# Spreading the FP4 quantizer over two engines step by step, and grouping the layer-norm apply of an MLP, in an eight-core transformer kernel

## The chip, the cores and the metric

The kernel runs on the 8 cores of one Trainium2 chip. Each core handles one of the 8 batch elements on its own, with no exchange between cores. The metric is the device time in microseconds (us) of the slowest core. Engines: PE (TensorE), DVE (VectorE), ACT (ScalarE), POOL (GpSimd), SP (SyncE, which here only issues transfers).

## What is computed

Two transformer layers on x of 2048 x 1024 per core. Layer 0 adds to x a differential attention and a gated FFN whose three products take FP4-quantized operands. Layer 1 adds a linear attention and a two-deep local-attention FFN block with an MLP. The parts that matter here are the quantizer, which runs on blocks of 16 values, and the layer norm ahead of each MLP:

```python
def fp4_quant_dequant(x):
    xb = x.reshape(shape[:-1] + (shape[-1] // 16, 16))
    scale = max(max(abs(xb)) / 6.0, 1e-12)          # one per block of 16
    idx = searchsorted(_MID, abs(xb / scale))       # grid 0 .5 1 1.5 2 3 4 6
    return (_GRID[idx] * sign(xb) * scale).reshape(shape)
# layer 0 FFN: everything that enters a product is quantized
gate = fp4(x) @ fp4(w_gate).T;  y = fp4(x) @ fp4(w_up).T
out  = fp4(silu(gate) * y) @ fp4(w_down).T
# layer 1, before each of the two MLPs (h is the token-shifted x)
h = (h - mu) / sqrt(var + 1e-5) * lg + lb
```

## The kernel before

The program is written by hand with counting semaphores. `Sem.inc` adds one when an instruction completes, `Sem.wait` makes an engine's queue wait until the count is reached, and `drain()` holds an engine's queue until its earlier instructions are done. The stages follow each other with barriers between them; within a stage most steps wait for the step before.

`emit_quant(k, S, Q)` (L266 to L320) quantizes one tile S of 128 x W into Q. It keeps three wide buffers, `qA`, `qB`, `qC` (each 128 x 2816 f32, used as f32 or as bf16 halves), and three short ones, `qbm`, `qib6`, `qbm12`, with one entry for each block of 16. In order: L275 DVE maximum of each block; L277 a floor on it; L279 reciprocal; L280 the block's scale (times 1/6); L282 the reciprocal times 6; L285 A = S times that; L287 B = A clamped to +-2; L288 C = A clamped to +-4; L291 POOL C + A; L293 A = 0.5 C + B; L296 z, rounded by adding and subtracting a large constant, in bf16; L301, L302, L303 three simple functions of z (m1, c6, z2); L305 m1 limited; L307 s1 = m1 + c6; L310 psi = z2 - s1; L317 POOL Q = psi times the block's scale. So two of the instructions are POOL's and sixteen are DVE's, with a DVE drain between dependent ones.

It is called 164 times:

- 16 times with W = 1024 in the loop over x tiles in `emit_l0`, then 16 PE transposes of the tile with its bf16 copy (`emit_transposes`, L330 PE, L332 DVE copy), then the next tile;
- 44 times with W = 1024 and 8 times with W = 2816 in `emit_l0_wquant` (weights). Each turn loads a row block (SP, L878), quantizes it, transposes it and stores it (L891); the next load waits for the stores' data to be ready and for DVE and POOL, and goes into the same buffer `WLD`;
- 80 times with W = 512 and 16 times with W = 256 in `emit_l0_ffn`. For each column chunk `oc` and row tile `j4` 16 matmuls (8 of L930, 8 of L933) are followed by a silu (ACT, L937), a product (DVE, L939), the quantizer into `HQB`, and 4 or 2 transposes. The next 16 matmuls wait for all of it.

Together that is 129,024 columns (60 x 1024 + 80 x 512 + 16 x 256 + 8 x 2816).

In `emit_l1f_mlp` (run for l = 0 and 1) the layer norm is applied for each half `hf` and each 512 columns `tc`: three short matmuls (L1687 to L1691) spread the mean and the scale of each token over the partitions in PSUM; then for each of 8 feature tiles `ft` DVE multiplies into a temporary T1 (L1696), DVE adds (L1699), and ACT applies gain and bias into `XHh` (L1702). DVE waits for ACT before the next `ft`, since T1 is one buffer. PE and POOL stand at a later barrier or wait.

Of the kernel before, what the change touches and what calls it, by code (L numbers as in the profile page):

```python
# [127 lines left out]
def full_barrier(k, engines="tvsg", dma=True):  # L128
    s = k.s_x
    if "t" in engines:  # L130
        s.inc(k.te.drain())
    if "v" in engines:
        s.inc(k.ve.drain())
    if "s" in engines:
        s.inc(k.se.drain())
    if "g" in engines:
        s.inc(k.ge.drain())
    for e in (k.te, k.ve, k.se, k.ge, k.sy):
        e.wait_ge(s.h, s.n)
        if dma and engines == "tvsg":  # L140
            for sem in (k.s_ld, k.s_la, k.s_lb, k.s_lg, k.s_lh, k.s_lc, k.s_st, k.s_dmp):
                sem.wait(e)
# [122 lines left out]

def emit_quant(k, S, Q, ge_q=True):  # L266
    v, g = k.ve, k.ge
    k.s_g.wait(v)
    W = S.shape[-1]
    nb = W // 16  # L270
    A, B, C = k.qA, k.qB, k.qC
    Ab, Bb, Cb = k.qAb, k.qBb, k.qCb
    bm, ib6, bm12 = k.qbm, k.qib6, k.qbm12
    S3 = S.rearrange("p (a b) -> p a b", b=16)
    v.tensor_reduce(bm[:, 0:nb], S3, axis=AX.X, op=ALU.max, apply_absolute_value=True)  # L275
    v.drain()
    v.tensor_scalar(bm[:, 0:nb], bm[:, 0:nb], 6e-12, None, op0=ALU.max)  # L277
    v.drain()
    v.reciprocal(ib6[:, 0:nb], bm[:, 0:nb])  # L279
    v.tensor_scalar(bm12[:, 0:nb], bm[:, 0:nb], k.rc6[:, 0:1], None, op0=ALU.mult)  # L280
    v.drain()
    v.tensor_scalar(ib6[:, 0:nb], ib6[:, 0:nb], 6.0, None, op0=ALU.mult)  # L282
    v.drain()
    ib6b = ib6[:, 0:nb].unsqueeze(2).broadcast_to((128, nb, 16))
    v.tensor_tensor(A[:, 0:W].rearrange("p (a b) -> p a b", b=16), S3, ib6b, op=ALU.mult)  # L285
    v.drain()
    v.tensor_scalar(B[:, 0:W], A[:, 0:W], -2.0, 2.0, op0=ALU.max, op1=ALU.min)  # L287
    v.tensor_scalar(C[:, 0:W], A[:, 0:W], -4.0, 4.0, op0=ALU.max, op1=ALU.min)  # L288
    k.s_v.inc(v.drain())  # L289
    k.s_v.wait(g)  # L290
    k.s_g.inc(g.tensor_tensor(C[:, 0:W], C[:, 0:W], A[:, 0:W], op=ALU.add))  # L291
    k.s_g.wait(v)
    v.scalar_tensor_tensor(A[:, 0:W], C[:, 0:W], 0.5, B[:, 0:W], op0=ALU.mult, op1=ALU.add)  # L293
    v.drain()
    z = Bb[:, 0:W]
    v.tensor_scalar(z, A[:, 0:W], k.mcol[:, 0:1], k.mcol[:, 0:1],  # L296
                    op0=ALU.add, op1=ALU.subtract)
    v.drain()
    m1, c6 = Cb[:, 0:W], Ab[:, 0:W]
    z2, s1 = Ab[:, W:2 * W], Cb[:, W:2 * W]  # L300
    v.tensor_scalar(m1, z, 0.5, -2.0, op0=ALU.mult, op1=ALU.max)  # L301
    v.tensor_scalar(c6, z, -6.0, 6.0, op0=ALU.max, op1=ALU.min)  # L302
    v.tensor_scalar(z2, z, 2.0, None, op0=ALU.mult)  # L303
    v.drain()
    v.tensor_scalar(m1, m1, 2.0, None, op0=ALU.min)  # L305
# [9 lines left out]
    if ge_q:
        k.s_v.wait(g)
        k.s_g.inc(g.tensor_tensor(Q3, psi3, bm12b, op=ALU.mult))  # L317
    else:
        v.tensor_tensor(Q3, psi3, bm12b, op=ALU.mult)
        k.s_v.inc(v.drain())  # L320


def emit_transposes(k, pairs, identity):
# [57 lines left out]
def emit_l0(k, h, out_h):  # L381
# [23 lines left out]
    for j in range(NT):  # L405
# [14 lines left out]
        k.s_v.wait(se)  # L420
        k.s_s.inc(se.activation(XB, XNT, AF.Copy, bias=0.0))
        emit_quant(k, XNT, XQT)
        if DEV_STAGE == "xq":
            k.s_g.wait(ge)
# [441 lines left out]
def emit_l0_wquant(k, h, WLD, WQB, STG):  # L866
    te, ve, se, ge, sy = k.te, k.ve, k.se, k.ge, k.sy
    specs = [(h["wg0"], h["wqgT_s"], 22, 1024),
             (h["wu0"], h["wquT_s"], 22, 1024),
             (h["wd0"], h["wdqT_s"], 8, 2816)]  # L870
    for src, dst, nrt, W in specs:
        srcr = src.rearrange("(r p) w -> p r w", p=128)
        dstr = dst.rearrange("(bb p) o -> p bb o", p=128)
        nb = W // 128
        for r in range(nrt):
            k.s_v.wait(sy)
            k.s_g.wait(sy)
# [236 lines left out]
def emit_l1_ffn(k, h, out_h, XINT):  # L1114
# [439 lines left out]
def emit_l1f_mlp(k, h, out_h, XINT, l, LNGC, LNBC, B1AC, B1GC, st4):  # L1554
    te, ve, se, ge, sy = k.te, k.ve, k.se, k.ge, k.sy
# [98 lines left out]
    w1src = h["w1"][l].rearrange("(a p) o -> p a o", p=128)  # L1654
    GH = k.qCb[:, 4096:4608]
    AT = k.qCb[:, 4608:5120]
    T1 = k.qCb[:, 5120:5632]

    for hf in range(2):
        ar.mark()  # L1660
        XHh = ar.bf(8, 1024)
        ar.mark()
        XFMh = ar.bf(8, 1032)
# [19 lines left out]
        for tc in range(2):  # L1683
            gcol = 1024 * hf + 512 * tc
            te.wait_ge(k.s_v.h, k.s_v.n)
            te.wait_ge(k.s_s.h, k.s_s.n)
            k.s_mm.inc(te.matmul(k.psB[:, 2, :], k.ones1b[0:1, 0:128],  # L1687
                                 IVB[0:1, gcol:gcol + 512], start=True, stop=True))
            te.matmul(k.psB[:, 3, :], k.ones1b[0:1, 0:128],
                      CHB[0:1, gcol:gcol + 512], start=True, stop=False)  # L1690
            k.s_mm.inc(te.matmul(k.psB[:, 3, :], k.ones1b[0:1, 0:128],  # L1691
                                 CLB[0:1, gcol:gcol + 512], start=False, stop=True))
            k.s_mm.wait(ve)
            for ft in range(8):
                soff = 1 if ft < 4 else 0
                ve.tensor_tensor(T1, XFMh[:, ft, soff + 512 * tc: soff + 512 * tc + 512],  # L1696
                                 k.psB[:, 2, :], op=ALU.mult)
                ve.drain()
                ve.tensor_tensor(T1, T1, k.psB[:, 3, :], op=ALU.add)  # L1699
                k.s_v.inc(ve.drain())  # L1700
                k.s_v.wait(se)
                k.s_s.inc(se.activation(XHh[:, ft, 512 * tc:512 * tc + 512], T1, AF.Identity,  # L1702
                                        scale=LNGC[:, ft:ft + 1], bias=LNBC[:, ft:ft + 1]))
                k.s_s.wait(ve)
        full_barrier(k, "tvs")
        ar.release()
        AHq = ar.bf(22, 512)
# [2 lines left out]
        for qt in range(2):  # L1710
# [3 lines left out]
            for hc in range(22):  # L1714
                ocw = 128 if hc < 21 else 42
                b = hc % 2
# [8 lines left out]
                for ag in range(2):  # L1725
                    for ic in range(8):
# [8 lines left out]
                              bias=B1GC[0:ocw, hc:hc + 1])  # L1735
                se.activation(AT[0:ocw, :], k.psA[0:ocw, 0, :], AF.Identity,
                              bias=B1AC[0:ocw, hc:hc + 1])
# [3 lines left out]
                                           op=ALU.mult))  # L1741
# [132 lines left out]
```

## Time and profile before

| | us |
|---|---|
| median of the runs shown (12597.27 to 12635.81) | 12616.54 |
| time of the profiled execution | 12579.73 |
| span of the profiled execution, slowest core | 12577.8 |
| busy: PE / DVE / ACT / POOL | 4373.9 / 3686.7 / 1556.9 / 1112.6 |

The eight cores span 12539.7 to 12577.8 us. No engine is busy for more than 35% of the span. The page has the busy time of each engine, the span in 40 slices, the transfer queues, the chain of work that ended last, and the costliest groups of instructions; the trace behind it can be asked for single stretches, lines and shapes.

### The profile page before, as it was taken

What the parts mean: (1) busy time and instruction counts of PE and PEld (TensorE: products, weight loads), DVE (VectorE), ACT (ScalarE), POOL (GpSimd) and SP (SyncE); (2) the same over time, 40 slices, a digit from 0 to 9 for tenths busy, and PEclk for the clock granted to TensorE, in tenths of its full rate; (3) what the DMA queues carried; (4) which work ended last, traced back from release to release, by engine and by line L of the source; (5) the groups of instructions that cost most, each with busy time, mean ns of one, the idle gap of its engine ahead of it and who ended that gap; (6) DMA issues with size and microseconds to landing.
All of it is one profiled execution on the core that took longest, in us unless ns stands there. A gap on an engine that the chain in (4) does not pass through costs nothing.

```text
span 12577.8 us, 70640 instructions; the slowest of 8 cores (12539.7 to 12577.8 us)
## 1 busy us (share of the span) xinstructions
PE 4373.9 (35%) x17918; PEld 1725.2 (14%) x18113; DVE 3686.7 (29%) x9617; ACT 1556.9 (12%) x2754; POOL 1112.6 (9%) x925
## 2 busy tenths in 40 slices
PE   1000033443444423333243333244446233244443
PEld 0000011111111111111121111111112011111111
DVE  6544533111111232332323544400100644400100
ACT  1000012333333100000011111100001111100100
POOL 1111210000000010110100000011111000011110
PEclk9999995555555666666666555577677555676676
DMA  1111110000000201011031000133233000233233
GB/s 52 30 36 35 43 33 1 0 0 0 0 0 0 65 20 44 29 35 37 27 87 58 6 0 1 27 32 34 23 31 28 2 1 0 31 30 32 27 29 69
DMA packets 563397, 326.69 MB, mean 26 GB/s; under 512 B 467046, under 2 KB 519398, under 8 KB 561980
## 3 DMA queue, kind: packets, MB, share of 16 engines
q0 software_dynamic: 406448, 125.85, 9.7%
q1 hardware_dynamic: 156564, 196.32, 4.8%
q8 instruction: 167, 2.74, 0.1%
q14 instruction: 218, 1.79, 0.0%
HBM read 388.63 MB, written 50.92 MB: 35 GB/s over the span
## 4 chain that ended last, share of the span: by engine, by line
PE 31%; DVE 22%; DMA 15%; issue 7%; POOL 7%; ACT 6%; ACTq 5%; DVEq 5%; SPq 0%; POOLq 0%; PEldq 0%
PE psA L1727 8%; DMA ARENA<-w 7%; PE psB L726 4%; ACTq L712 3%; PE psB L1755 3%; PE psA L930 2%; POOL qC L291 2%; DVE qB L1388 2%; PE psA L933 2%; DMA ARENA<-wquT_s 2%; DMA ARENA<-x_s 2%; POOL ARENA L1740 2%; DVE ARENA L1481 1%; ACT ARENA L711 1%; PE psB L1479 1%
## 5 line engine op out<-in xcount | busy, mean ns | idle before, releaser
L1727 PE MATMUL psA<-ARENA 128*128 128x512 bf16 (+1 forms) x2760 | 963.5, 522 | 1647.1 <-DMA ARENA<-w 1639.8
L330 PE MATMUL psA<-c_idb,ARENA 128*128 128x128 bf16 x1424 | 244.3, 264 | 1948.5 <-POOL ARENA L317 1605.0
L1761 DVE TENSOR_TENSOR ARENA<-ARENA,psB 128x512 bf16<-128x512 bf16 x64 | 41.1, 684 | 2891.3 <-PE psB L1755 2891.3
L726 PE MATMUL psB<-ARENA 128*65 128x512 bf16 (+3 forms) x1280 | 522.2, 562 | 825.3 <-ACTq L712 509.2
L711 ACT ACTIVATE ARENA<-psA 128x512 bf16<-128x512 f32 (+3 forms) x1280 | 578.9, 539 | 920.5 <-PE psA L703 920.2
L1727 PEld LDWEIGHTS psA<-ARENA 128*128 128x128 bf16 (+1 forms) x2816 | 343.7, 127 | 2267.5 <-issue 2170.8
L291 POOL TENSOR_TENSOR qC<-qC,qA 128x512 f32<-128x512 f32 (+3 forms) x164 | 301.4, 1838 | 2409.4 <-DVEq L289 2409.4
L717 DVE TENSOR_TENSOR ARENA<-ARENA,c_m 128x512 bf16<-128x512 bf16 x128 | 54.5, 426 | 1553.8 <-ACTq L712 1553.8
L1479 PE MATMUL psB<-c_idb,ARENA 128*128 128x128 bf16 x1120 | 226.1, 270 | 654.8 <-DVEq L1469 504.0
L330 PE MATMUL psA<-c_idb,qC 128*128 128x128 bf16 x352 | 60.2, 265 | 1066.0 <-POOL qC L317 1065.8
L330 PEld LDWEIGHTS psA<-c_idb,ARENA 128*128 128x128 bf16 x1424 | 148.5, 104 | 2045.4 <-issue 2009.7
L1734 ACT ACTIVATE qC<-psA,B1GC 128x512 bf16<-128x512 f32 (+1 forms) x176 | 120.9, 687 | 2481.1 <-PE psA L1727 2481.1
L332 DVE COPY ARENA<-psA 128x128 bf16<-128x128 bf16 x1776 | 288.3, 221 | 444.0 <-PE psA L330 415.9
L930 PE MATMUL psA<-ARENA 128*128 128x512 bf16 (+1 forms) x752 | 303.1, 576 | 301.8 <-DMA ARENA<-wquT_s 262.3
L1740 POOL TENSOR_TENSOR ARENA<-qC 128x512 bf16<-128x512 bf16 (+1 forms) x176 | 201.2, 1143 | 2224.2 <-ACTq L1738 2224.2
L1755 PE MATMUL psB<-ARENA 128*128 128x512 bf16 (+1 forms) x1376 | 332.6, 391 | 3.0 <-issue 1.6
L726 PEld LDWEIGHTS psB<-ARENA 128*65 128x65 bf16 x1280 | 170.6, 162 | 1186.4 <-issue 1175.3
L1460 ACT ACTIVATE ARENA<-psA,stats 128x640 bf16<-128x640 f32 (+4 forms) x256 | 172.1, 723 | 1136.2 <-DVEq L1456 1136.2
L939 DVE TENSOR_TENSOR qA<-qA,psA 128x512 f32<-128x512 f32 (+1 forms) x96 | 61.7, 643 | 833.0 <-ACT qA L937 833.0
L937 ACT ACTIVATE qA<-psA 128x512 f32<-128x512 f32 (+1 forms) x96 | 53.9, 561 | 1987.8 <-PE psA L933 1987.8
L1481 DVE COPY ARENA<-psB 128x128 bf16<-128x128 bf16 x1120 | 206.7, 221 | 236.1 <-PE psB L1479 232.3
L293 DVE SCALAR_TENSOR_TENSOR qA<-qC,qB 128x512 f32<-128x512 f32 (+3 forms) x164 | 160.5, 978 | 349.0 <-POOL qC L291 349.0
(345 smaller groups left out, 7236.7 us busy)
## 6 DMA issues: line engine op xcount, KB each, us to landing
ARENA<-w POOLq DMA_DIRECT2D x336, 256.0 KB, 4.7
ARENA<-x_s SPq DMA_DIRECT2D x80, 512.0 KB, 3.6
x_s<-ARENA SPq DMA_DIRECT2D x48, 512.0 KB
ARENA<-wqgT_s SPq DMA_DIRECT2D x20, 1024.0 KB, 5.5
ARENA<-wquT_s SPq DMA_DIRECT2D x20, 1024.0 KB, 8.0
ARENA<-x_in SPq DMA_DIRECT2D x32, 512.0 KB, 3.9
ARENA<-wg SPq DMA_DIRECT2D x22, 512.0 KB, 4.0
ARENA<-wu SPq DMA_DIRECT2D x22, 512.0 KB, 4.0
```

Source lines behind the costliest of these rows:

```text
L291: k.s_g.inc(g.tensor_tensor(C[:, 0:W], C[:, 0:W], A[:, 0:W], op=ALU.add))
L330: k.s_mm.inc(k.te.transpose(pv, src, identity))
L332: k.s_v.inc(ve.tensor_copy(dst, pv))
L711: se.activation(UT[:, jj, off:512], k.psA[:, jj, off:512], AF.Exp)
L712: k.s_s.inc(se.drain())
L726: k.s_mm.inc(te.matmul(k.psB[0:65, jj, off:512], VT[:, kt, kvv, 0:65], UT[:, jj, off:512], start=(kt == 0), stop=(kt == nkt - 1)))
L930: te.matmul(k.psA[:, 0, 0:ocw], XQF[:, ic, 128 * j:128 * j + 128], WGS[:, ic, 0:ocw], start=(ic == 0), stop=(ic == 7))
L1479: k.s_mm.inc(te.transpose(pvb, UT[:, jj, 128 * b:128 * b + 128], k.idb[:]))
L1481: k.s_v.inc(ve.tensor_copy(UTT[:, jj, ktr, 128 * lq:128 * lq + 128], pvb))
L1727: mm = te.matmul(k.psA[0:ocw, ag, :], W1S[:, ag, b, ic, 0:ocw], XHh[:, ic, toff:toff + 512], start=(ic == 0), stop=(ic == 7))
L1740: k.s_g.inc(ge.tensor_tensor(AHq[0:ocw, hc, :], AT[0:ocw, :], GH[0:ocw, :], op=ALU.mult))
L1755: mm = te.matmul(pb, AHq[0:kcw, hc, 128 * tch:128 * tch + 128], W2R[0:kcw, hc, 512 * dc:512 * dc + 512], start=False, stop=(hc == 21))
```

## The change

In `emit_quant` the steps go to DVE and POOL in turn. Each step waits for the other engine's last one and signals its own completion directly; the DVE drains inside are gone. The floor, the block scale, B, m1, z2 and s1 move from DVE to POOL; the multiplication of the reciprocal by 6 is folded into the instruction that makes A; and a POOL memset of one column is put in to keep the turns. s1 moves from `qC`'s second half to `qB`'s. In the MLP's layer norm the eight `ft` are handled in three passes (8 multiplies, 8 adds, 8 ACT instructions) through `XHh` in place of T1.

```diff
-    v.tensor_reduce(bm[:, 0:nb], S3, ...)
-    v.drain()
-    v.tensor_scalar(bm[:, 0:nb], bm[:, 0:nb], 6e-12, None, op0=ALU.max)
...
+    def vstep(fn):
+        v.wait_ge(k.s_g.h, k.s_g.n)
+        k.s_v.inc(fn())
+    def gstep(fn):
+        g.wait_ge(k.s_v.h, k.s_v.n)
+        k.s_g.inc(fn())
+    vstep(lambda: v.tensor_reduce(bm[:, 0:nb], S3, axis=AX.X, op=ALU.max,
+                                  apply_absolute_value=True))
+    gstep(lambda: g.tensor_scalar(bm[:, 0:nb], bm[:, 0:nb], 6e-12, None, op0=ALU.max))
+    vstep(lambda: v.reciprocal(ib6[:, 0:nb], bm[:, 0:nb]))
+    gstep(lambda: g.tensor_scalar(bm12[:, 0:nb], bm[:, 0:nb], 1.0 / 6.0, None, op0=ALU.mult))
+    vstep(lambda: v.scalar_tensor_tensor(A, S3, 6.0, ib6b, op0=ALU.mult, op1=ALU.mult))
+    gstep(lambda: g.tensor_scalar(B[:, 0:W], A[:, 0:W], -2.0, 2.0, op0=ALU.max, op1=ALU.min))
+    vstep(lambda: v.tensor_scalar(C[:, 0:W], A[:, 0:W], -4.0, 4.0, op0=ALU.max, op1=ALU.min))
+    gstep(lambda: g.tensor_tensor(C[:, 0:W], C[:, 0:W], A[:, 0:W], op=ALU.add))
+    vstep(lambda: v.scalar_tensor_tensor(A[:, 0:W], C[:, 0:W], 0.5, B[:, 0:W], ...))
+    gstep(lambda: g.memset(k.smallc[:, 14:15], 0.0))
+    vstep(lambda: v.tensor_scalar(z, A[:, 0:W], k.mcol[:, 0:1], k.mcol[:, 0:1], ...))
+    gstep(lambda: g.tensor_scalar(m1, z, 0.5, -2.0, op0=ALU.mult, op1=ALU.max))
+    vstep(lambda: v.tensor_scalar(c6, z, -6.0, 6.0, op0=ALU.max, op1=ALU.min))
+    gstep(lambda: g.tensor_scalar(z2, z, 2.0, None, op0=ALU.mult))
+    vstep(lambda: v.tensor_scalar(m1, m1, 2.0, None, op0=ALU.min))
+    gstep(lambda: g.tensor_tensor(s1, m1, c6, op=ALU.add))
+    vstep(lambda: v.tensor_tensor(psi, z2, s1, op=ALU.subtract))
+    gstep(lambda: g.tensor_tensor(Q3, psi3, bm12b, op=ALU.mult))
...
             for ft in range(8):
-                ve.tensor_tensor(T1, XFMh[...], k.psB[:, 2, :], op=ALU.mult)
-                ve.drain()
-                ve.tensor_tensor(T1, T1, k.psB[:, 3, :], op=ALU.add)
-                k.s_v.inc(ve.drain())
-                k.s_v.wait(se)
-                k.s_s.inc(se.activation(XHh[...], T1, AF.Identity, scale=..., bias=...))
-                k.s_s.wait(ve)
+                ve.tensor_tensor(XHh[...], XFMh[...], k.psB[:, 2, :], op=ALU.mult)
+            ve.drain()
+            for ft in range(8):
+                ve.tensor_tensor(XHh[...], XHh[...], k.psB[:, 3, :], op=ALU.add)
+            k.s_v.inc(ve.drain())
+            k.s_v.wait(se)
+            for ft in range(8):
+                se.activation(XHh[...], XHh[...], AF.Identity, scale=..., bias=...)
+            k.s_s.inc(se.drain())
+            k.s_s.wait(ve)
+            k.s_s.wait(te)
```

## Rows read from the trace of the kernel before

**Rows 1.** Busy time by stage (windows): weight quantizing, then one FFN group of four tiles.

```profile
core 6: us, PE busy (x) PEld busy (x) DVE busy (x) ACT busy (x) POOL busy (x), PEclk, DMA share, GB/s
385.00:1357.00 972.00, 59.28 (x352) 36.64 (x352) 483.33 (x1056) 0.00 (x0) 186.84 (x88) 1.00 0.12 35
4300.00:4840.00 540.00, 185.00 (x636) 75.48 (x648) 171.70 (x504) 14.76 (x25) 54.99 (x52) 0.63 0.13 36
```

**Rows 2.** Timeline of one W = 1024 quantizing: start us, us, engine, line.

```profile
519.56 1.22 DVE L275 TENSOR_REDUCE qbm<-ARENA 128x64 f32<-128x1024 f32 x1 [5.08 <-DMA ARENA<-wg]
...
521.12 0.55 DVE L279 RECIPROCAL qib<-qbm 128x64 f32<-128x64 f32 x1
...
522.10 1.23 DVE L285 TENSOR_TENSOR qA<-ARENA,qib 128x1024 f32<-128x1024 f32 x1
523.40 0.69 DVE L287 TENSOR_SCALAR qB<-qA 128x1024 f32<-128x1024 f32 x1
524.01 0.69 DVE L288 TENSOR_SCALAR qC<-qA 128x1024 f32<-128x1024 f32 x1
524.87 2.34 POOL L291 TENSOR_TENSOR qC<-qC,qA 128x1024 f32<-128x1024 f32 x1 [12.63 <-DVEq L289]
527.31 1.23 DVE L293 SCALAR_TENSOR_TENSOR qA<-qC,qB 128x1024 f32<-128x1024 f32 x1 [2.62 <-POOL qC L291]
...
529.50 0.43 DVE L301 TENSOR_SCALAR qC<-qB 128x1024 bf16<-128x1024 bf16 x1
...
530.68 0.43 DVE L305 TENSOR_SCALAR qC<-qC 128x1024 bf16<-128x1024 bf16 x1
531.18 0.69 DVE L307 TENSOR_TENSOR qC<-qC,qA 128x1024 bf16<-128x1024 bf16 x1
531.95 0.69 DVE L310 TENSOR_TENSOR qC<-qA,qC 128x1024 bf16<-128x1024 bf16 x1
532.81 1.91 POOL L317 TENSOR_TENSOR ARENA<-qC,qbm 128x1024 bf16<-128x1024 bf16 x1 [5.61 <-DVEq L311]
```

**Rows 3.** Groups by shape, POOL's two lines: xcount, busy us, mean ns, idle before.

```profile
L317 POOL TENSOR_TENSOR ARENA<-qC,qbm 128x1024 bf16<-128x1024 bf16 x60 | 114.6, 1909 | 337.3 <-DVEq L311 337.3
L317 POOL TENSOR_TENSOR qC<-qC,qbm 128x512 bf16<-128x512 bf16 x80 | 83.7, 1046 | 300.6 <-DVEq L311 300.6
L291 POOL TENSOR_TENSOR qC<-qC,qA 128x2816 f32<-128x2816 f32 x8 | 48.9, 6108 | 205.8 <-DVEq L289 205.8
L317 POOL TENSOR_TENSOR ARENA<-qC,qbm 128x2816 bf16<-128x2816 bf16 x8 | 39.5, 4932 | 97.5 <-DVEq L311 97.5
```

**Rows 4.** Groups by shape, two of DVE's clamping lines at W = 2816.

```profile
L287 DVE TENSOR_SCALAR qB<-qA 128x2816 f32<-128x2816 f32 x8 | 13.0, 1627 | 0.6
L301 DVE TENSOR_SCALAR qC<-qB 128x2816 bf16<-128x2816 bf16 x8 | 7.2, 894 | 0.6
```

**Rows 5.** Timeline: a DVE copy that releases POOL directly, and POOL's one-output iota.

```profile
6773.21 0.21 DVE L1195 COPY E2B<-psA 2x128 bf16<-2x128 bf16 x1 [0.55 <-PE psA L1193]
6773.56 1.84 POOL L1201 IOTA qA<- 128x2048 f32 x1 [3.46 <-DVE E2B L1195]
```

**Rows 6.** Timeline of the first layer-norm apply (512 columns, eight feature tiles).

```profile
8091.06 0.69 DVE L1696 TENSOR_TENSOR qC<-ARENA,psB 128x512 bf16<-128x512 bf16 x1 [1.79 <-PE psB L1691]
...
8093.56 0.69 DVE L1696 TENSOR_TENSOR qC<-ARENA,psB 128x512 bf16<-128x512 bf16 x1 [1.04 <-ACT ARENA L1702]
...
8110.08 0.81 ACT L1702 ACTIVATE ARENA<-qC,LNBC,LNGC 128x512 bf16<-128x512 bf16 x1 [1.68 <-DVEq L1700]
```

**Rows 7.** Timeline: four DVE products in a row, and four ACT instructions in a row.

```profile
7032.63 2.48 DVE L1398 TENSOR_TENSOR ARENA<-ARENA,psA 128x512 bf16<-128x512 bf16 x4 [2.14 <-PE psA L1394]
```

```profile
2339.00 2.06 ACT L711 ACTIVATE ARENA<-psA 128x512 bf16<-128x512 f32 x4 [3.29 <-PE psA L703]
```

**Rows 8.** Timeline of PE in one FFN burst of 16 matmuls.

```profile
4516.47 3.57 PE L930 MATMUL psA<-ARENA 128*128 128x512 bf16 x8 [0.48 <-DVE ARENA L332]
4519.84 2.05 PE L933 MATMUL psA<-ARENA 128*128 128x512 bf16 x8
```

**Rows 9.** PE in two stretches of that burst: busy us (xcount), granted clock, DMA.

```profile
4516.50:4519.50 3.00, 3.00 (x8) 0.50 0.00 0
4520.00:4522.00 2.00, 1.89 (x9) 0.96 0.00 0
```

More of the change, by code:

```diff
@@ L267, in emit_quant @@
     v, g = k.ve, k.ge
-    k.s_g.wait(v)
     W = S.shape[-1]
@@ L274, in emit_quant @@
     S3 = S.rearrange("p (a b) -> p a b", b=16)
-    v.tensor_reduce(bm[:, 0:nb], S3, axis=AX.X, op=ALU.max, apply_absolute_value=True)
-    v.drain()
-    v.tensor_scalar(bm[:, 0:nb], bm[:, 0:nb], 6e-12, None, op0=ALU.max)
[L278 to L283, printed above, removed]
-    ib6b = ib6[:, 0:nb].unsqueeze(2).broadcast_to((128, nb, 16))
@@ L285, in emit_quant @@
[L285 to L293, printed above, removed]
@@ L294, in emit_quant @@
-    v.drain()
-    z = Bb[:, 0:W]
[L296 to L305, printed above, removed]
@@ L306, in emit_quant @@
-    v.drain()
-    v.tensor_tensor(s1, m1, c6, op=ALU.add)
-    v.drain()
+    def vstep(fn):
[8 more added lines that the diff above has]
+    vstep(lambda: v.reciprocal(ib6[:, 0:nb], bm[:, 0:nb]))
@@ new lines, in emit_quant @@
+    gstep(lambda: g.tensor_scalar(bm12[:, 0:nb], bm[:, 0:nb], 1.0 / 6.0, None, op0=ALU.mult))
+    ib6b = ib6[:, 0:nb].unsqueeze(2).broadcast_to((128, nb, 16))
+    vstep(lambda: v.scalar_tensor_tensor(A[:, 0:W].rearrange("p (a b) -> p a b", b=16),
+                                         S3, 6.0, ib6b, op0=ALU.mult, op1=ALU.mult))
+    gstep(lambda: g.tensor_scalar(B[:, 0:W], A[:, 0:W], -2.0, 2.0, op0=ALU.max, op1=ALU.min))
+    vstep(lambda: v.tensor_scalar(C[:, 0:W], A[:, 0:W], -4.0, 4.0, op0=ALU.max, op1=ALU.min))
@@ new lines, in emit_quant @@
+    gstep(lambda: g.tensor_tensor(C[:, 0:W], C[:, 0:W], A[:, 0:W], op=ALU.add))
+    vstep(lambda: v.scalar_tensor_tensor(A[:, 0:W], C[:, 0:W], 0.5, B[:, 0:W],
+                                         op0=ALU.mult, op1=ALU.add))
+    gstep(lambda: g.memset(k.smallc[:, 14:15], 0.0))
+    z = Bb[:, 0:W]
+    vstep(lambda: v.tensor_scalar(z, A[:, 0:W], k.mcol[:, 0:1], k.mcol[:, 0:1],
+                                  op0=ALU.add, op1=ALU.subtract))
+    m1 = Cb[:, 0:W]
+    c6 = Ab[:, 0:W]
+    z2 = Ab[:, W:2 * W]
@@ L309, in emit_quant @@
+    s1 = Bb[:, W:2 * W]
+    gstep(lambda: g.tensor_scalar(m1, z, 0.5, -2.0, op0=ALU.mult, op1=ALU.max))
[3 more added lines that the diff above has]
+    gstep(lambda: g.tensor_tensor(s1, m1, c6, op=ALU.add))
     psi = Cb[:, 0:W]
-    v.tensor_tensor(psi, z2, s1, op=ALU.subtract)
-    k.s_v.inc(v.drain())
+    vstep(lambda: v.tensor_tensor(psi, z2, s1, op=ALU.subtract))
@@ L314, in emit_quant @@
     psi3 = psi.rearrange("p (a b) -> p a b", b=16)
[L315 to L320, printed above, removed]
+    gstep(lambda: g.tensor_tensor(Q3, psi3, bm12b, op=ALU.mult))
 def emit_transposes(k, pairs, identity):
@@ L1656, in emit_l1f_mlp @@
     AT = k.qCb[:, 4608:5120]
-    T1 = k.qCb[:, 5120:5632]
     for hf in range(2):
@@ L1695, in emit_l1f_mlp @@
                 soff = 1 if ft < 4 else 0
-                ve.tensor_tensor(T1, XFMh[:, ft, soff + 512 * tc: soff + 512 * tc + 512],
+                ve.tensor_tensor(XHh[:, ft, 512 * tc:512 * tc + 512],
+                                 XFMh[:, ft, soff + 512 * tc: soff + 512 * tc + 512],
                                  k.psB[:, 2, :], op=ALU.mult)
-                ve.drain()
-                ve.tensor_tensor(T1, T1, k.psB[:, 3, :], op=ALU.add)
-                k.s_v.inc(ve.drain())
-                k.s_v.wait(se)
-                k.s_s.inc(se.activation(XHh[:, ft, 512 * tc:512 * tc + 512], T1, AF.Identity,
-                                        scale=LNGC[:, ft:ft + 1], bias=LNBC[:, ft:ft + 1]))
-                k.s_s.wait(ve)
+            ve.drain()
+            for ft in range(8):
+                ve.tensor_tensor(XHh[:, ft, 512 * tc:512 * tc + 512],
+                                 XHh[:, ft, 512 * tc:512 * tc + 512],
+                                 k.psB[:, 3, :], op=ALU.add)
+            k.s_v.inc(ve.drain())
+            k.s_v.wait(se)
+            for ft in range(8):
+                se.activation(XHh[:, ft, 512 * tc:512 * tc + 512],
+                              XHh[:, ft, 512 * tc:512 * tc + 512], AF.Identity,
+                              scale=LNGC[:, ft:ft + 1], bias=LNBC[:, ft:ft + 1])
+            k.s_s.inc(se.drain())
+            k.s_s.wait(ve)
+            k.s_s.wait(te)
         full_barrier(k, "tvs")
```

## Prediction

> **What bounds the kernel now.** I read first the page's busy shares and its 40 slices, to see whether an engine is full. None is. Then the windows by stage: while the weights are quantized DVE is busy for 483 of 972 us and POOL for 187; in an FFN group PE has 185 of 540 us, DVE 172, POOL 55 [rows 1]. The stages are chains in which one engine works at a time. Then the timeline of one quantizing, which the reader should follow row by row: DVE works from 519.56 to 524.70, POOL to 527.21, DVE to 532.64, POOL to 534.72, and no two rows overlap by more than the tail of a DVE instruction [rows 2]. This piece is 15.16 us long. The code says what stands around it: the transposes wait for Q, the next load into the one buffer WLD or the next 16 matmuls wait for the transposes. Nothing is prepared meanwhile, so whatever a quantizing gains or loses goes 164 times straight into the end.
>
> **Boundaries.** From one DVE instruction over a drain to the next takes 0.07 us (L305 ends at 531.11, L307 starts at 531.18). DVE through a drain to POOL takes 0.17 (L288 ends 524.70, L291 starts 524.87), POOL to DVE 0.10 (527.21 to 527.31) [rows 2]. A DVE instruction that releases POOL by itself, as the new code has it, is shown once: 0.14 (6773.42 to 6773.56) [rows 5].
>
> **The quantizer, W = 1024.** I count what leaves, what comes, and the boundaries.
>
> Leaving DVE: the floor L277, 521.12 - 519.56 - 1.22 - 0.07 = 0.27. L280 and L282, 522.10 - 521.12 - 0.55 - 0.07 = 0.36. B (L287), 524.01 - 523.40 = 0.61. m1 and z2: from L301 to L305 is 1.18, of which c6 with a boundary keeps 0.49, so 0.69. s1 (L307), 531.95 - 531.18 = 0.77 [rows 2]. Together 2.70.
>
> Coming to POOL: s1 has L317's shape and types, 1.91 [rows 2]. The other five have no row: nowhere does POOL run an operation with one input and a constant. What is known of POOL is two-input work: 4932 ns at 2816 columns and 1909 at 1024, so 1.69 ns a column and 0.18 us fixed in bf16; 6108 and 2340 in f32, so 2.10 ns a column and the same 0.18 [rows 2, 3]; and work with no input, iota, (1.84 - 0.18) / 2048 = 0.81 ns a column [rows 5]. These are the bounds of a one-input operation. I take half the two-input rate, 1.05 ns in f32 and 0.84 in bf16: it reads half as much, and the result lies next to iota, which shows that POOL's writing and looping can go at that pace. Then B costs 0.18 + 1.08 = 1.26, m1 and z2 1.04 each, the two on 64 columns 0.25 each, the memset the fixed 0.18. With s1: 1.26 + 2.08 + 0.50 + 0.18 + 1.91 = 5.93.
>
> The Trainium skill (GPSIMD Engine Reference, section 3.1) gives a port-bound POOL loop of up to two operations 1.03 cycles an element, and a tight loop otherwise 1.8; at the 1.2 GHz it states these are 0.86 and 1.5 ns. By the first the term below for all calls would be some 25 us smaller, by the second some 230 us larger (estimates from that page). No row here shows either.
>
> Boundaries: before, between the instructions that stay, seven of 0.07, two of 0.17, one of 0.10, 0.93 in all. After, 18 instructions in strict turns have 17: nine DVE to POOL at 0.14 and eight back at 0.10, 2.06. That is 1.13 more. Dropping drains thus gains nothing; a turn costs more than a drain.
>
> The balance is 5.93 - 2.70 + 1.13 = +4.36 us a quantizing. No cover exists for it: each POOL step is waited for by the next DVE step, even where the data don't ask for it (B and C could run side by side, and so could m1, c6 and z2), and behind DVE's waits stand the transposes' copies.
>
> **Other widths.** Per column come 1.05 + 0.84 + 0.84 + 1.69, and 2 x 1.05 / 16 for the short ones: 4.55 ns. Per column leave (1627 - 694) / 1792 = 0.52 for B and the same for s1, (894 - 427) / 1792 = 0.26 each for m1 and z2 [rows 2, 4], and 3 x 0.52 / 16 = 0.10: 1.66 ns. The net is 2.89 ns a column, and per call 4.36 - 1024 x 0.00289 = 1.40 us. Over 164 calls and 129,024 columns: 230 + 373 = +603 us.
>
> **The layer norm.** Eight feature tiles take 8110.89 - 8091.06 = 19.83 us, 2.50 each [rows 6]. After, a pass of 8 DVE instructions goes at (2.48 - 0.69) / 3 = 0.60 from start to start [rows 7]: 7 x 0.60 + 0.69 = 4.89, twice, with a drain 9.85, then 0.17 to ACT. ACT's steps lie between 0.51 (2.06 / 4) [rows 7] and the 0.81 of a lone one [rows 6]; with 0.70, 0.81 + 7 x 0.70 = 5.7. That is 15.7, or -4.1 us, and there are 8 such pieces (2 layers, 2 halves, 2 chunks): -33 us (-43 to -27). PE waits for this stretch before and after, so the gain counts in full; the added wait on PE is for work that it needed anyway. What follows is the barrier and the first weight load, which start that much sooner.
>
> **Sum.** +603 - 33 = +570 us. The profiled execution took 12579.7, so it would take 13150; the median of the runs shown is 37 us above it, so I say 12616.5 + 570, rounded to 13185.
>
> **Rivals.**
>
> 1. POOL's one-input operations go no faster than its two-input ones, because the pace is set by its loop and not by what it reads. Then B costs 1.05 ns a column more, m1 and z2 0.85 each, the short ones 0.13: 2.88 x 129,024 = +371, in all +941, 13560 us. For it speaks that the f32 and bf16 rates differ by less than the bytes do (2.10 against 1.69) [rows 2, 3]; against it that iota shows a pace of 0.81. The skill's 1.8 cycles would lie between this and my value. 24%.
>
> 2. The clock. An FFN burst starts at a granted clock of 0.50 (the 1.2 GHz level) and reaches 0.96 (2.4 GHz nearly throughout) in its second half [rows 9]. If the longer pause of PE kept the low level through the burst, its 16 matmuls would take 16 x 3.37 / 8 = 6.7 us in place of 5.42 [rows 8], 1.3 x 80 = +105 us, 13290. Against it: the clock is already at the low level when the burst starts, so 2.7 us more of pause have nothing to take away. 8%.
>
> 3. The other side, not slower: POOL does what it is given at DVE's price, s1 included. Then 0.69 + 0.43 + 0.42 + 0.69 + 0.36 for the short ones + 0.18 come, 2.77, and the balance is 2.77 - 2.70 + 1.13 = 1.20 us a call with hardly a part per column: 197 - 33 = +164, 12780 us, within 2%. It would need the total below +252 (2%). With only B, m1 and z2 at DVE's rates the total is still 570 - (0.53 + 0.58 + 0.58) x 129,024 / 1000 = +352, so the decision lies with s1, and POOL's 1.91 for that shape is a row [rows 3]. 4%.
>
> That the quantizer is not on the path, so that only the -33 remains, is excluded by rows 2: DVE's next row waits for each POOL row.
>
> **How the numbers follow.** 62% for my case, with a spread of its own: low end, all at iota's pace (-39), every boundary 0.10 (-59), memset free (-30), layer norm -43: 13050; high end, pieces of rival 1. 24, 8 and 4% for the rivals, 2% for something unseen. The range is 13040 to 13560, from just below my low end up to rival 1 (with boundaries of 0.17 that one would reach 13610). It leaves out rival 3 and the far edge of rival 1. 2% is about what a measurement of this kernel can tell from no change. Slower by over 2%: 0.94, within 2%: 0.05, faster: 0.01.
>
> **What would show it.** After: six POOL lines more, each in a gap of DVE's; the time from block maximum to Q at W = 1024 about 19.5 us; POOL clamp of 1024 f32 columns 1.26 us (2.34 by rival 1, 0.69 by rival 3); bursts in the FFN that still end at the high clock; layer-norm pieces of 15.7 us. POOL's busy time should rise by some 800 us and DVE's fall by some 400. I am wrong if the clamp's price is far from 1.26, or if a turn costs much else than 0.10 to 0.14.

## The result and the profile after

The changed kernel takes 14077.29 us in the median (14036.59 to 14144.68) against 12605.12 for the kernel before: a ratio of 1.1164, 95% interval 1.1131 to 1.1196. That is +1472 us, where +570 was forecast, and outside the range. The direction and the place were right, the size was not.

First the stretches, which answer to [rows 1]. The same core, 6, in both kernels: weight quantizing from its first quantizer to the first projection matmul, the FFN, and everything from the first layer-norm piece to the end. Columns are the stretch, its length, busy us (and count) of PE, PE's weight loads, DVE, ACT, POOL, then the granted clock and the transfers.

Kernel before:

```profile
65.00:1786.00 1721.00, 132.96 (x784) 81.59 (x784) 921.39 (x1904) 23.49 (x21) 346.90 (x139) 1.00 0.13 37
4311.00:6494.00 2183.00, 734.52 (x2544) 301.65 (x2592) 706.35 (x2038) 75.07 (x131) 222.40 (x211) 0.64 0.13 38
8091.00:12578.00 4487.00, 1810.43 (x6532) 706.59 (x6633) 792.68 (x2075) 450.19 (x702) 524.20 (x545) 0.67 0.25 26
```

Kernel after:

```profile
62.00:2711.00 2649.00, 132.80 (x784) 81.72 (x784) 733.09 (x1428) 23.49 (x21) 1395.62 (x615) 1.00 0.08 24
5211.00:7959.00 2748.00, 711.47 (x2544) 296.88 (x2592) 559.66 (x1366) 75.09 (x131) 865.56 (x883) 0.63 0.11 30
9557.00:13998.00 4441.00, 1799.14 (x6532) 705.21 (x6633) 781.19 (x2075) 444.63 (x702) 524.73 (x545) 0.67 0.25 26
```

The two stretches with the quantizer grew by 928 and 565 us, 1493 together; on the other seven cores, cut at the same instructions, by 1496 to 1529. In the first, POOL's busy time rose by 1049 us and DVE's fell by only 188. That makes 861, and the hand-overs add some 77 (68 calls of 1.13 us each, an estimate by the prediction's count): the stretch grew by 928, since nobody works beside POOL.

The last stretch shrank by 46 on this core, but it can't be read as the layer norm's gain. On cores 4 to 7 it shrank by 43 to 50 us, at a granted clock of 0.67 (0.66 to 0.67 before); on cores 0 to 3 it grew by 10 to 32, at 0.65 (0.66 to 0.67 before). What the layer norm gives is shown by its pieces below and by e1_ln_alone.

Then one W = 1024 quantizing of the kernel after, which answers to [rows 2] (start us, us, engine, line; in brackets the idle time before it and who ended it):

```profile
571.75 1.22 DVE L283 TENSOR_REDUCE qbm<-ARENA 128x64 f32<-128x1024 f32 x1 [4.03 <-DMA ARENA<-wg]
573.13 0.37 POOL L285 TENSOR_SCALAR qbm<-qbm 128x64 f32<-128x64 f32 x1 [8.90 <-DVE qbm L283]
...
576.17 3.63 POOL L291 TENSOR_SCALAR qB<-qA 128x1024 f32<-128x1024 f32 x1 [1.48 <-DVE qA L289]
579.91 0.69 DVE L292 TENSOR_SCALAR qC<-qA 128x1024 f32<-128x1024 f32 x1 [3.89 <-POOL qB L291]
580.75 2.34 POOL L293 TENSOR_TENSOR qC<-qC,qA 128x1024 f32<-128x1024 f32 x1 [0.95 <-DVE qC L292]
583.19 1.23 DVE L294 SCALAR_TENSOR_TENSOR qA<-qC,qB 128x1024 f32<-128x1024 f32 x1 [2.59 <-POOL qC L293]
584.54 0.10 POOL L296 MEMSET smallc<- 128x1 f32 x1 [1.45 <-DVE qA L294]
584.75 0.81 DVE L298 TENSOR_SCALAR qB<-qA,c_mcol 128x1024 bf16<-128x1024 f32 x1 [0.33 <-POOL smallc L296]
585.72 3.63 POOL L304 TENSOR_SCALAR qC<-qB 128x1024 bf16<-128x1024 bf16 x1 [1.08 <-DVE qB L298]
589.46 0.43 DVE L305 TENSOR_SCALAR qA<-qB 128x1024 bf16<-128x1024 bf16 x1 [3.90 <-POOL qC L304]
590.04 2.77 POOL L306 TENSOR_SCALAR qA<-qB 128x1024 bf16<-128x1024 bf16 x1 [0.69 <-DVE qA L305]
...
593.50 2.11 POOL L308 TENSOR_TENSOR qB<-qC,qA 128x1024 bf16<-128x1024 bf16 x1 [0.68 <-DVE qC L307]
595.72 0.69 DVE L310 TENSOR_TENSOR qC<-qA,qB 128x1024 bf16<-128x1024 bf16 x1 [2.37 <-POOL qB L308]
596.55 1.91 POOL L314 TENSOR_TENSOR ARENA<-qC,qbm 128x1024 bf16<-128x1024 bf16 x1 [0.94 <-DVE qC L310]
```

From 571.75 to 598.46 it is 26.71 us, against 15.16. The reader should look at three durations, 3.63, 3.63 and 2.77 us for B, m1 and z2, and then at the bracket of the DVE row behind each (3.89, 3.90 and 3.03): DVE stands for that time and the two hand-overs. The turns are as expected: 0.15 us from DVE to POOL (580.60 to 580.75), 0.10 back (583.09 to 583.19).

The groups by shape give POOL's price at W = 2816 (count, busy us, mean ns, idle before):

```profile
L291 POOL TENSOR_SCALAR qB<-qA 128x2816 f32<-128x2816 f32 x8 | 77.4, 9675 | 26.8 <-DVE qA L289 26.8
L306 POOL TENSOR_SCALAR qA<-qB 128x2816 bf16<-128x2816 bf16 x8 | 58.5, 7310 | 9.5 <-DVE qA L305 9.5
L308 POOL TENSOR_TENSOR qB<-qC,qA 128x2816 bf16<-128x2816 bf16 x8 | 43.9, 5492 | 9.2 <-DVE qC L307 9.2
```

With the 1024 rows: (9675 - 3630) / 1792 = 3.37 ns a column for two operations, (7310 - 2770) / 1792 = 2.53 for one, both above the 2.10 of two-input f32 work [rows 2, 3].

Last the first layer-norm piece, which answers to [rows 6]:

```profile
9611.74 4.87 DVE L1689 TENSOR_TENSOR ARENA<-ARENA,psB 128x512 bf16<-128x512 bf16 x8 [1.79 <-PE psB L1684]
9616.69 4.87 DVE L1694 TENSOR_TENSOR ARENA<-ARENA,psB 128x512 bf16<-128x512 bf16 x8
9621.69 5.74 ACT L1700 ACTIVATE ARENA<-ARENA,LNBC,LNGC 128x512 bf16<-128x512 bf16 x8 [50.46 <-DVEq L1697]
```

It ends at 9627.43, 15.69 us after its start, as forecast (15.7), with each of its three terms in place.

### The profile page after: what moved, and what is told of

Read it like the earlier page. It is cut to its first block, busy times and chain, and to the rows that moved or that the text cites. A ratio compares the mean times of both kernels' runs of the same rounds, so it can differ in the third digit from the quotient of the medians.

```text
span 14143.1 us, 70955 instructions; the slowest of 8 cores (13997.7 to 14143.1 us)
## 1 busy us (share of the span) xinstructions
PE 4485.3 (32%) x18113; PEld 1742.9 (12%) x18113; DVE 3339.6 (24%) x8469; ACT 1551.9 (11%) x2754; POOL 2802.2 (20%) x2073
## 4 chain that ended last, share of the span: by engine, by line
PE 29%; POOL 18%; DVE 18%; DMA 13%; issue 7%; ACTq 5%; ACT 5%; DVEq 4%; POOLq 0%; SPq 0%; PEldq 0%
PE psA L1728 7%; DMA ARENA<-w 6%; PE psB L720 4%; POOL qC L304 3%; POOL qB L291 3%; ACTq L706 3%; PE psB L1756 3%; POOL qA L306 3%; POOL qC L293 2%; PE psA L924 2%; POOL qB L308 2%; DVE qB L1382 1%; POOL ARENA L1741 1%; DMA ARENA<-wquT_s 1%; DMA ARENA<-x_s 1%
## 5 line engine op out<-in xcount | busy, mean ns | idle before, releaser
L1728 PE MATMUL psA<-ARENA 128*128 128x512 bf16 (+1 forms) x2816 | 1001.4, 534 | 1618.0 <-DMA ARENA<-w 1618.0
L291 POOL TENSOR_SCALAR qB<-qA 128x512 f32<-128x512 f32 (+3 forms) x164 | 466.2, 2843 | 204.0 <-DVE qA L289 204.0
L304 POOL TENSOR_SCALAR qC<-qB 128x512 bf16<-128x512 bf16 (+3 forms) x164 | 466.8, 2846 | 158.4 <-DVE qB L298 158.4
L285 POOL TENSOR_SCALAR qbm<-qbm 128x32 f32<-128x32 f32 (+3 forms) x164 | 54.4, 331 | 1842.7 <-DVE qbm L283 1842.7
L924 PE MATMUL psA<-ARENA 128*128 128x512 bf16 (+1 forms) x768 | 298.8, 566 | 297.1 <-DMA ARENA<-wquT_s 260.6
L306 POOL TENSOR_SCALAR qA<-qB 128x512 bf16<-128x512 bf16 (+3 forms) x164 | 357.7, 2181 | 104.0 <-DVE qA L305 104.0
L1756 PE MATMUL psB<-ARENA 128*128 128x512 bf16 (+1 forms) x1408 | 372.6, 423 | 0.0
```

The lines of the kernel that those rows point to most:

```text
L291: gstep(lambda: g.tensor_scalar(B[:, 0:W], A[:, 0:W], -2.0, 2.0, op0=ALU.max, op1=ALU.min))
L304: gstep(lambda: g.tensor_scalar(m1, z, 0.5, -2.0, op0=ALU.mult, op1=ALU.max))
L306: gstep(lambda: g.tensor_scalar(z2, z, 2.0, None, op0=ALU.mult))
L924: te.matmul(k.psA[:, 0, 0:ocw], XQF[:, ic, 128 * j:128 * j + 128], WGS[:, ic, 0:ocw], start=(ic == 0), stop=(ic == 7))
L1728: mm = te.matmul(k.psA[0:ocw, ag, :], W1S[:, ag, b, ic, 0:ocw], XHh[:, ic, toff:toff + 512], start=(ic == 0), stop=(ic == 7))
L1756: mm = te.matmul(pb, AHq[0:kcw, hc, 128 * tch:128 * tch + 128], W2R[0:kcw, hc, 512 * dc:512 * dc + 512], start=False, stop=(hc == 21))
```

## The experiments

Theory P: the excess is what POOL asks for one-input operations. Theory T: it is the price of handing every step over. All ratios are to the kernel before, timed on the same chip as the experiment.

### The layer norm alone (e1_ln_alone)

```diff
 # emit_quant as before; only the layer norm is the changed kernel's
```

> The quantizer of before with the grouped layer norm of after. The changed kernel's trace has one layer-norm piece at 15.69 us against 19.83 before. If nothing takes that back, eight pieces give -33 us: about 12572 against a before of 12605, ratio 0.997. Rival: the gain is lost in the weight loads and the barrier behind it, ratio 1.000.

Measured: 12544.71 against 12575.67 us, ratio 0.997 (0.9954 to 0.9986). The gain is real: the interval is 18 to 58 us, and the 33 read from the timeline lie in it. So what stands behind the layer norm did not take all of it back.

### Turns without moving any work (e2_turns)

The edit, shortened:

```diff
-    v.drain()                       # ten times in emit_quant
+    k.s_v.inc(last)                 # last: the DVE instruction before
+    g.wait_ge(k.s_v.h, k.s_v.n)
+    k.s_g.inc(g.memset(k.smallc[:, 14:15], 0.0))
+    v.wait_ge(k.s_g.h, k.s_g.n)
```

> The kernel before, except that each of the 10 DVE drains inside the quantizer is replaced by a turn over POOL (DVE releases POOL, POOL sets one column to zero, DVE waits for it). Every computing instruction stays on its engine. Theory P (the loss of the change is what POOL asks for one-input operations): a turn costs 0.14 + 0.10 + 0.10 us in place of 0.07, so 10 x 0.27 x 164 = +440 us, ratio about 1.035. Theory T (the loss of about 1500 us is the price of the turns, 17 a call, so 0.54 us each): 10 x 0.54 x 164 = +885 us, ratio about 1.07.

Measured: 12989.11 us, ratio 1.0335 (1.0313 to 1.0357). Its timeline around A (L291 there) and B (L293):

```profile
551.58 1.23 DVE L291 TENSOR_TENSOR qA<-ARENA,qib 128x1024 f32<-128x1024 f32 x1 [0.32 <-POOL smallc L277]
552.93 0.10 POOL L277 MEMSET smallc<- 128x1 f32 x1 [1.45 <-DVE qA L291]
553.13 0.69 DVE L293 TENSOR_SCALAR qB<-qA 128x1024 f32<-128x1024 f32 x1 [0.32 <-POOL smallc L277]
```

From the end of A (552.81) to B is 0.32 us where a drain took 0.07. Ten times 164 times 0.25 is 410 us, and 0.0335 x 12576 is 421. A turn has the price that the rows of before gave it (0.14 + 0.10 for the hand-overs). Theory T, which needed 1.07, is out.

### One-input work back on DVE, turns kept (e3_one_input_on_dve)

The edit, shortened:

```diff
-    gstep(lambda: g.tensor_scalar(B[:, 0:W], ...))
+    gstep(lambda: g.memset(k.smallc[:, 14:15], 0.0))
+    v.wait_ge(k.s_g.h, k.s_g.n)
+    v.tensor_scalar(B[:, 0:W], ...)      # m1 and z2 likewise, ahead of c6
```

> The changed kernel with B, m1 and z2 back on DVE; where they stood POOL sets one column to zero, so the number of turns is the same. Theory P: at W = 1024 POOL's 3.63 + 3.63 + 2.77 us give way to 0.61 + 0.34 + 0.34 on DVE and three times 0.10, -8.4 us; over all widths about -1070 us, to 13010, ratio 1.032 to before. Theory T: the turns are all still there, so it stays within some 300 us of the changed kernel, ratio 1.09 or more.

Measured: 12979.82 us, ratio 1.0319 (1.0302 to 1.0337), the figure of theory P. Three of POOL's instructions, taken away with all the turns left standing, return 1.1164 - 1.0319 = 0.0845 of the time of before, some 1065 of the 1472 us. This one and e2_turns settle where the time went.

### What POOL charges (e4_prices, e8_prices2)

In both, lone POOL operations, nearly all on 128 x 1024, are put ahead of the changed kernel; nothing reads their results. Six of e4_prices' fifteen, with the lines they have in the profile:

```diff
+    gs(lambda: g.tensor_scalar(c, a, -2.0, 2.0, op0=ALU.max, op1=ALU.min))   # L1832
+    gs(lambda: g.tensor_scalar(c, a, -2.0, None, op0=ALU.max))               # L1833
+    gs(lambda: g.tensor_scalar(c, a, 2.0, None, op0=ALU.mult))               # L1834
+    gs(lambda: g.tensor_scalar(c, a, 2.0, 1.0, op0=ALU.mult, op1=ALU.add))   # L1835
+    gs(lambda: g.tensor_copy(c, a))                                          # L1836
...
+    gs(lambda: g.tensor_tensor(c, a, a, op=ALU.add))                         # L1839
...
```

> The changed kernel with a list of lone POOL operations on 128 x 1024 ahead of it (three times each, some 110 us longer for it). From 3.37 ns a column with two operations and 2.53 with one: if each arithmetic operation costs 0.84 ns on top of a base, a plain copy costs 0.18 + 1.7 = 1.9 us, a lone max and a lone multiply both 2.77, and f32 and bf16 the same. Rival: what is paid for is the way of the instruction (a constant operand), then a copy goes at iota's 0.8 ns a column, 1.0 us, and only instructions with constants are slow. z + z as a two-input sum: about 2.1 us in bf16 against 2.77 for z times 2.

Groups by shape of e4_prices:

```profile
L1832 POOL TENSOR_SCALAR qC<-qA 128x1024 f32<-128x1024 f32 x3 | 10.9, 3623 | 22.7 <-DVEq L133 22.4 <-POOL qC L1832 0.3
L1834 POOL TENSOR_SCALAR qC<-qA 128x1024 f32<-128x1024 f32 x3 | 8.3, 2769 | 0.5 <-POOL qC L1834 0.3 <-POOL qC L1833 0.2
L1833 POOL TENSOR_SCALAR qC<-qA 128x1024 f32<-128x1024 f32 x3 | 8.3, 2764 | 0.5 <-POOL qC L1833 0.3 <-POOL qC L1832 0.2
...
L1839 POOL TENSOR_TENSOR qC<-qA 128x1024 f32<-128x1024 f32 x3 | 5.7, 1891 | 0.4
...
L1835 POOL TENSOR_SCALAR qC<-qA 128x1024 f32<-128x1024 f32 x3 | 3.1, 1045 | 0.5 <-POOL qC L1835 0.3 <-POOL qC L1834 0.2
L1836 POOL COPY qC<-qA 128x1024 f32<-128x1024 f32 x3 | 3.1, 1039 | 0.4
```

A lone max and a lone multiply cost the same 2.77 us; max and min together 3.62. But multiply and add together cost 1.04, less than the multiply alone, and as much as a copy. So neither the expectation (a base and 0.84 ns for each operation, a copy of 1.9 us) nor its rival (every instruction with a constant is slow) held. The second list, given here in words, looks for the bounds of the quick case:

```text
op0, op1 on f32 unless said:  L1831 mult, mult    L1832 add, mult
L1833 add, add    L1834 mult, subtract    L1835 mult, max
L1836 add    L1837 min    L1838 mult, add in bf16    L1839 the same, f32 to bf16
L1840 mult, add on 2816 columns    L1841 mult by a constant held in memory
```

> The changed kernel with a second list of lone POOL operations ahead of it. If only multiply then add is quick, the pairs mult-mult, add-mult, add-add, mult-subtract take 3.6 us and lone add and min 2.77; if all pairs without max or min are quick, they take 1.04. Multiply and add in bf16, f32 to bf16, and on 2816 f32 columns: 1.04, 1.04 and 2.6 us (0.84 ns a column) if the quick way does not depend on type. A constant taken from memory in place of the instruction: 2.77, as the lone multiply.

```profile
L1834 POOL TENSOR_SCALAR qC<-qA 128x1024 f32<-128x1024 f32 x3 | 10.9, 3634 | 0.5 <-POOL qC L1834 0.3 <-POOL qC L1833 0.2
L1833 POOL TENSOR_SCALAR qC<-qA 128x1024 f32<-128x1024 f32 x3 | 10.9, 3632 | 0.5 <-POOL qC L1833 0.3 <-POOL qC L1832 0.2
...
L1840 POOL TENSOR_SCALAR qC<-qA 128x2816 f32<-128x2816 f32 x3 | 7.6, 2538 | 0.5 <-POOL qC L1840 0.3 <-POOL qC L1839 0.2
...
L1838 POOL TENSOR_SCALAR qC<-qA 128x1024 bf16<-128x1024 bf16 x3 | 3.1, 1045 | 0.5 <-POOL qC L1838 0.3 <-POOL qC L1837 0.2
...
L1832 POOL TENSOR_SCALAR qC<-qA 128x1024 f32<-128x1024 f32 x3 | 3.1, 1043 | 0.5 <-POOL qC L1832 0.3 <-POOL qC L1831 0.2
L1831 POOL TENSOR_SCALAR qC<-qA 128x1024 f32<-128x1024 f32 x3 | 3.1, 1040 | 19.7 <-DVEq L133 19.4 <-POOL qC L1831 0.3
```

Quick are multiply-add, multiply-multiply and add-multiply in f32, and multiply-add in bf16 too (the other two were not tried in it); from the two widths of multiply-add, (2538 - 1045) / 1792 = 0.83 ns a column. Slow at 3.6 us are add-add and multiply-subtract, and multiply-max, which is m1's pair (3626 ns here). Lone add and min cost 2.77, a lone multiply by a constant from memory 2.84. Both parts of the expectation missed: it is not the pair multiply then add alone, and it is not all pairs without max or min. Why it is these three pairs is left open.

### The quick pair in the kernel (e7_z2_mult_add)

```diff
-    gstep(lambda: g.tensor_scalar(z2, z, 2.0, None, op0=ALU.mult))
+    gstep(lambda: g.tensor_scalar(z2, z, 2.0, 0.0, op0=ALU.mult, op1=ALU.add))
```

> The changed kernel with one edit: POOL makes z2 as z times 2 plus 0 (two operations) where it made z times 2 (one). If POOL's lone multiply and add pair is quick in bf16 as it was in f32 (1.04 us at 1024 columns, against 2.77 for the lone multiply), -1.73 us at W = 1024 and about -220 us in all, ratio 1.099. If the price goes by the number of operations, it becomes 3.63 us and the kernel 110 us longer, ratio 1.125.

Measured: 13859.13 us, ratio 1.1026 (1.0992 to 1.106). z2 at W = 1024:

```profile
L306 POOL TENSOR_SCALAR qA<-qB 128x1024 bf16<-128x1024 bf16 x60 | 62.8, 1047 | 41.6 <-DVE qA L305 41.6
```

An addition of zero takes z2 from 2771 to 1047 ns, and over all widths POOL's time for z2 from 357.7 to 139.2 us. The difference of the ratios, 0.0138, is 174 us with about 60 either way; the 220 expected is within that.

### Waits only where data ask (e5_data_waits)

The edit in words:

```diff
-    vstep / gstep in strict turns
+    each instruction on the engine it has in the changed kernel, but
+    B (POOL) beside C (DVE), bm12 beside the reciprocal, m1 beside c6,
+    z2 beside the limit on m1; no memset
```

> The changed kernel with every instruction on the engine that the change gave it, but with waits only where data ask for them, so that B runs beside C, the block scale beside the reciprocal, m1 beside c6, z2 beside the limit on m1; the memset is gone. From the rows of the changed kernel that hides at W = 1024 some 0.95 + 0.58 + 0.69 + 0.69 us and saves 0.28, -3.2 us; over all widths about -480 us, so 13600, ratio 1.08. Rival: a DVE instruction and a POOL instruction do not run side by side (the later one stands until the first is done), then only the turns are saved, about -150 us, ratio 1.105. In the trace: whether C (0.69 us alone) ends long before B or with it.

Measured: 13703.05 us, ratio 1.0889 (1.0858 to 1.092): 0.0275, or 347 us, come back, not 480. The engines do run side by side, but not freely:

```profile
598.11 0.69 DVE L296 TENSOR_SCALAR qC<-qA 128x1024 f32<-128x1024 f32 x1
598.16 4.13 POOL L294 TENSOR_SCALAR qB<-qA 128x1024 f32<-128x1024 f32 x1 [1.58 <-DVE qA L291]
...
610.81 2.77 POOL L312 TENSOR_SCALAR qA<-qB 128x1024 bf16<-128x1024 bf16 x1
610.95 1.18 DVE L316 TENSOR_SCALAR qC<-qC 128x1024 bf16<-128x1024 bf16 x1 [3.60 <-POOL qC L310]
```

B, started 0.05 us behind C, takes 4.13 us and not 3.63. The limit on m1, started behind z2, takes 1.18 and not 0.43. The one that starts second pays. How much it pays depends on the width. At W = 2816 the same pair of z2 and the limit on m1 reads:

```profile
2492.95 7.30 POOL L312 TENSOR_SCALAR qA<-qB 128x2816 bf16<-128x2816 bf16 x1
2493.08 7.92 DVE L316 TENSOR_SCALAR qC<-qC 128x2816 bf16<-128x2816 bf16 x1 [9.64 <-POOL qC L310]
```

By the Trainium skill (SBUF — State Buffer, section "Who interferes with whom") the ports that POOL shares with a DVE instruction in a 2-port mode go to whoever issues first, and the second "fully blocks" for the whole instruction. At W = 2816 this agrees: DVE's instruction (0.89 us alone) takes 7.92 and ends 0.75 us behind POOL's. POOL behind DVE agrees too: B grows by 0.49 us behind a C of 0.69 and by 1.44 behind one of 1.63, each time some 0.15 us less than the rest of DVE's instruction. But at W = 1024 DVE's ended 1.45 us ahead of POOL's, so there it did not wait for the whole of it. Why the narrower tile gets through is left open.

POOL's B and m1 are longer by 60 and 27 us over all calls, and s1 stands 7 us more behind the limit on m1. That is some 95 of the missing 133 us; the rest is within the interval.

### Everything on DVE (e6_all_on_dve), and Q alone on POOL (e9_q_on_pool)

```diff
-    k.s_g.inc(g.tensor_tensor(C[:, 0:W], C[:, 0:W], A[:, 0:W], op=ALU.add))
+    v.tensor_tensor(C[:, 0:W], C[:, 0:W], A[:, 0:W], op=ALU.add)
...
-    k.s_g.inc(g.tensor_tensor(Q3, psi3, bm12b, op=ALU.mult))
+    v.tensor_tensor(Q3, psi3, bm12b, op=ALU.mult)      # by ge_q=False; not in e9_q_on_pool
...
+    # the factor 6 folded into A; the layer norm as in the changed kernel
```

> The quantizer of before with all of it on DVE (C + A and Q too, the factor 6 folded into the instruction that makes A), with the grouped layer norm of after. At W = 1024 2.61 us from C to the next DVE step become 1.37, Q with its hand-over 2.4 become 1.1, the fold saves 0.27: -2.8 us; over all widths -374, with the layer norm -407 us, so 12190, ratio 0.968. If POOL's two steps cost little more than on DVE, only the layer norm and the fold would show: ratio 0.994.

> The kernel with the quantizer on DVE and the grouped layer norm, but with the last step Q left on POOL as before. In the all-DVE kernel DVE's Q took 1.23 us at W = 1024 and PE's first transpose started 1.58 us after psi, against 2.44 in the kernel before; at W = 512 1.04 against 1.58. So Q on POOL costs 0.86 x 60 + 0.54 x 80 and some 20 us for the other widths, +115 us on the all-DVE kernel: about 12370, ratio 0.983. If moving C + A was the whole gain, it stays at 0.974.

Measured: all on DVE 12252.96 us, ratio 0.9738 (0.9713 to 0.9763); with Q on POOL 12335.6, ratio 0.9802 (0.9768 to 0.9836). The first beats both kernels. It gains 330 us (298 to 361) and not 407, and the timeline shows why:

```profile
515.67 1.23 DVE L289 TENSOR_TENSOR qC<-qC,qA 128x1024 f32<-128x1024 f32 x1
...
522.37 1.23 DVE L317 TENSOR_TENSOR ARENA<-qC,qbm 128x1024 bf16<-128x1024 bf16 x1
```

C + A costs 1.23 us in place of POOL's 2.34 and its two hand-overs. Q costs 1.23 too, where s1's 0.69 was assumed for it: its second input is one bf16 value repeated 16 times. That is 0.54 x 60 + 0.26 x 80 and about 13 us for the other widths, 66 of the missing 77. For e9_q_on_pool the expected ratio, 0.983, lies in the interval, and 0.974 does not: Q on DVE is still worth something, 0.6% (0.2 to 1.1%). Of the 2.0% that remain with Q on POOL, the layer norm has 0.3% (e1_ln_alone); the rest is C + A and the dropped multiplication by 6, which no run separates.

## Why the prediction was wrong, point by point

**What bounds the kernel.** Right. All of the quantizer's growth, 1493 us in its two stretches, appears in the total: with -33 for the layer norm it makes +1460, against +1472 measured. Nothing covered POOL.

**Turns.** Right: 0.15 and 0.10 read, 0.14 and 0.10 used; e2_turns gives their cost by itself.

**What leaves DVE, and s1.** Right within little: s1 took 2.11 us, not 1.91. The value of L317 was not that of its shape in general, since L317 reads one input as a repeated value; that is some 26 us.

**The five one-input operations.** This is the step that failed: "I take half the two-input rate", 1.05 and 0.84 ns a column, and still more the sentence before it, "These are the bounds of a one-input operation". They reason from what an instruction reads, and B and m1 cost 3.37 ns a column, z2 2.53. The page of the kernel after has the three long ones:

```profile
L291 POOL TENSOR_SCALAR qB<-qA 128x512 f32<-128x512 f32 (+3 forms) x164 | 466.2, 2843 | 204.0 <-DVE qA L289 204.0
L304 POOL TENSOR_SCALAR qC<-qB 128x512 bf16<-128x512 bf16 (+3 forms) x164 | 466.8, 2846 | 158.4 <-DVE qB L298 158.4
L306 POOL TENSOR_SCALAR qA<-qB 128x512 bf16<-128x512 bf16 (+3 forms) x164 | 357.7, 2181 | 104.0 <-DVE qA L305 104.0
```

1290.7 us, where the sum had 165 + 138 + 138 = 441 (164 times 0.18 us plus 1.05 and twice 0.84 ns on 129,024 columns). That is 850 us short. The two short ones took 109 and not 77, s1 273 and not 248, the memset 16 and not 30. Together 895; 603 + 895 = 1498, and the two stretches grew by 1493 to 1529, by core.

**Rival 1** was right that what POOL reads does not set the pace: the clamp costs 3.62 us on f32 and on bf16, and the pair of multiply and add reads as much for 1.04. It was wrong in making the two-input rate its ceiling: one input with two constants is dearer (3.37 ns a column) than two inputs (2.10). An upper bound that is only the dearest row seen is no bound for a kind of instruction that has no row. The same holds for the two figures of the Trainium skill (GPSIMD Engine Reference, section 3.1) for a POOL loop, which I weighed in the prediction: they bracketed 0.86 to 1.5 ns, and the clamp took 3.37. Its 1.03 cycles (0.86 ns) come near the measured 0.83 ns, but of the one-input operations tried only the copy and the three quick pairs go at that pace.

**Rival 2, the clock,** did not come. The FFN's matmuls did not get longer though PE paused longer before each burst (565 us over 96 calls, 5.9 us each): 566 ns (L924, 576 before) and 423 (L927, 440 before).

**Rival 3** fell with the same rows: the clamp took 3.63 us on POOL, where DVE's took 0.69.

**The layer norm.** Right in each term; the total of e1_ln_alone agrees within its interval.

## What to carry to other kernels

In a chain where one engine works at a time, moving a step to an idle engine changes the time by the difference of the two engines' prices plus the hand-over; that the engine was idle gives nothing back unless something runs beside it. Price a kind of instruction that the trace does not show by measuring it, with its very operations; if that can't be done, leave the range open upwards rather than close it at the dearest neighbour. And look first at what already sits on the slow engine: here taking POOL out of the chain was worth most of 2.6%, of which the layer norm has 0.3.

## What the runs showed of the hardware

- A one-input POOL operation costs 2.77 us on 128 x 1024 with one operation and 3.63 with two, f32 and bf16 alike where both were tried; multiply-add, multiply-multiply and add-multiply cost 1.04. A copy costs 1.04, a two-input sum 2.34 in f32 and 2.11 in bf16, and 1.89 if both inputs are the same tile (e4_prices, e8_prices2).
- With one input a repeated value, a bf16 product at 1024 columns is quicker on POOL (1.91 against 2.11) and slower on DVE (1.23 against 0.69 for a sum or difference of two plain inputs).
- DVE and POOL side by side (e5_data_waits): the second to start is held up. POOL behind DVE grew by 0.49 us at 1024 columns and 1.44 at 2816; DVE behind POOL by 0.75 at 1024, and at 2816 it took 7.92 us in place of 0.89.
- A hand-over between DVE and POOL by the instructions themselves, there and back, costs 0.25 us; a DVE drain 0.07.
